# The product that subtracts the row maximum issued ahead of one projection piece or tail product in each quarter of a turn

## The chip, the cores and the metric

The kernel runs on one core of one Trainium2 chip. The metric is the device time of the whole program in microseconds (us), the median of several executions.

## The reference, cut to what matters

Two blocks are added to a residual stream of 16 x 256 tokens with 128 channels. The part that this case is about is the stack of six local-attention layers in the first block:

```python
for i in range(DEPTH):                       # DEPTH = 6, HEADS = 16, DIM_HEAD = 64, WINDOW = 32
    x = attn_layer(shift_tokens(x), Wqkv[i], q_scale[i], k_scale[i], Wo[i]) + x
    x = ffn_layer(shift_tokens(x), ln_g[i], ln_b[i], W1[i], b1[i], W2[i], b2[i]) + x

# attn_layer
q, k, v = jnp.split(x @ Wqkv, 3, -1)         # per head: q, k normalised, scaled, rotated
sim = jnp.einsum('bhwie,bhwje->bhwij', bq, bk2) * QK_SCALE      # window of 32 against 64 keys
sim = jnp.where(mask, -jnp.finfo(sim.dtype).max, sim)
attn = jax.nn.softmax(sim, -1)
out = jnp.einsum('bhwij,bhwje->bhwie', attn, bv2)
```

The softmax subtracts the maximum of each row before the exponential. The rest (a feature-map attention before these layers, a linear attention and eight experts behind them) is computed by other phases of the kernel, which the change doesn't touch.

## The kernel before

**Phases.** `features_phase`, then `layers_phase`, then the mixing and experts phase. `layers_phase` is written by hand in raw engine queues: each engine executes its list in order, and semaphores tie the lists together. A wait stands in front of the instruction that needs it, so everything behind it on the same engine waits too.

**Turns and quarters.** `turns` runs `turn(layer, j)` for 6 layers x 16 batches, 96 turns in steady work, with a few turns at the start and at the end that are partly empty. A turn works on several batches at once: it projects batch j+1, attends for batch j (and the tail of j-1), and runs the feed-forward of batches j-2 and j-3. It has four quarters; each handles one "group" (128 queries x 8 heads) at three stages of attention. I number the quarters 0 to 3, as the index of `gs`, `gt` and `ga` in the code.

**What PE does in a quarter.** `score` (L295 mask product, L304 the score products) for group gs, `probs_t` (L321) for group ga, `q_t` (L277) for group gt, then one piece of other work, then `shift` (L312) for gs, `pv` (L333) for ga, `k_t` (L286) for gt, `out_t` (L342) for ga, and between them further pieces. The piece that stands between `q_t` and `shift` is

- quarter 0: `k0`, six projection products (L221 to L223),
- quarter 1: `q1`, six projection products, and `mean` (L366),
- quarter 2: `hidden2`, two products of the feed-forward (L388),
- quarter 3: `wo_first`, the first half of the output projection (L351). It waits for `resid2`, which DVE raises in `finish` (L862).

**How the row maximum travels.** DVE's `row_max` (L762) waits for the scores and writes the negated maxima `neg_max`. PE's `shift` waits for it (`nmax`) and adds them to the scores in PSUM with a product against the identity. ACT's `exps` (L540) waits for `shifted`. The probabilities are used one quarter later, by `probs_t` and by DVE's `row_sum` (L768). `pv` in the same quarter belongs to the previous group; it needs `probs_t_out` (ACT, L547), not this quarter's exponential.

**DVE's order in a quarter.** `cosines` (L738, waits for ACT's squares L502), in quarter 1 also `normalize` (L849), `row_max`, in quarter 3 `finish` (L862), in quarter 2 two `glu` (L855), then `row_sum`, `sines` (L748), `norm_out` (L778, waits for `pv`), `sum_squares` (L756). At the end of the turn stands the Newton chain for reciprocal square roots (`newton`) and `rstd_diag` (L825). At the turns next to the end of a layer, `divide` (L714 to L716) splits the next layer's weights on DVE as well.

Of the kernel before, what the change touches and what calls it, by code (L numbers as in the profile page):

```python
# [43 lines left out]
def after(eng, sem, count):  # L44

    if not isinstance(count, int) or count > 0:
        eng.wait_ge(sem, count)
# [19 lines left out]
def layers_phase(nc, layer_qk, layer_w, consts, XF):  # L67

    ctx = ExitStack()
    with ctx:  # L70
# [75 lines left out]
        def more(layer):  # L146

            return not isinstance(layer, int) or layer < DEPTH - 1
# [64 lines left out]
        def _(pe):  # L213
            mm = nc.tensor.matmul

            def project(m, t, x, bank, done):

                for half in range(2):
                    out, o = bank[:, 512 * half:512 * half + 512], x * INNER + 512 * half
                    hi, lo = XHI[m.p][:, t * P:(t + 1) * P], XLO[m.p][:, t * P:(t + 1) * P]  # L220
                    mm(out, hi, HI[:, o:o + 512], start=True, stop=False)  # L221
                    mm(out, hi, LO[:, o:o + 512], start=False, stop=False)  # L222
                    last = mm(out, lo, HI[:, o:o + 512], start=False, stop=True)  # L223
                last.then_inc(done, 1)
# [9 lines left out]
            def k0(m):  # L234

                if m.live:
                    after(pe, rot, m.n * 8)
                    project(m, 0, 1, PJ[1], proj_qk)

            def q1(m):  # L240

                if m.live:
                    pe.wait_ge(rot, m.n * 8 + 2)
                    after(pe, v_out, m.n * 2)
                    project(m, 1, 0, PJ[0], proj_qk)
# [9 lines left out]
            def v0(m):  # L255

                if m.live:
                    pe.wait_ge(rot, m.n * 8 + 6)
                    project(m, 0, 2, PJ[0], proj_v)
# [10 lines left out]
            def q_t(g):  # L270

                if g.live:
                    pe.wait_ge(scaled, g.n + 1)
                    after(pe, kt_out, g.n * 2)
                    for c in range(4):
                        o = (4 * g.half + c) * P
                        last = nc.tensor.transpose(TP[:, c * P:(c + 1) * P], U[g.m.p][:, g.t, 0, o:o + P], IDENT[:])  # L277
                    last.then_inc(tq_mm, 1)

            def k_t(g):  # L280

                if g.live:
                    pe.wait_ge(qt_out, g.n + 1)
                    for c in range(4):
                        o = (4 * g.half + c) * P
                        last = nc.tensor.transpose(TP[:, c * P:(c + 1) * P], U[g.m.p][:, g.t, 1, o:o + P], IDENT[:])  # L286
                    last.then_inc(tk_mm, 1)

            def score(g):

                if not g.live:
                    return
                base = TILE0 - WIN if g.t == 0 else HALO
                after(pe, exped, g.n)
                mm(S[:].rearrange("p (c k) -> p c k", k=P), IDR[:], MASKR[:, g.t:g.t + 1, :].broadcast_to([P, 4, P]), start=True, stop=False,  # L295
                   skip_group_check=True)
                pe.wait_ge(qt_out, g.n + 1)
                pe.wait_ge(kt_out, g.n * 2 + 2)
                if g.t == 1:
                    pe.wait_ge(halo, g.m.n * 2 + g.half + 1)  # L300
                for c in range(4):
                    for w in range(4):
                        q, k = g.t * P + WIN * w, base + WIN * w
                        last = mm(S[WIN * w:WIN * w + WIN, c * P:(c + 1) * P], QT[:, 4 * g.half + c, q:q + WIN],  # L304
                                  KD[:, :, 4 * g.half + c, k:k + 2 * WIN], start=False, stop=True, skip_group_check=True)
                last.then_inc(scores, 1)

            def shift(g):

                if g.live:  # L310
                    pe.wait_ge(nmax, g.n + 1)
                    mm(S[:].rearrange("p (a e) -> p a e", e=DH), IDR[:], NMX[:].unsqueeze(2).broadcast_to((P, 8, DH)), start=False, stop=True,  # L312
                       skip_group_check=True).then_inc(shifted, 1)

            def probs_t(g):

                if g.live:
                    pe.wait_ge(exped, g.n + 1)
                    after(pe, ot_out, g.n)
                    for c in range(4):  # L320
                        last = nc.tensor.transpose(A[:, c * P:(c + 1) * P], E[:, g.k % 2, c * P:(c + 1) * P], IDENT[:])  # L321
                    last.then_inc(pt_mm, 1)

            def pv(g):

                if not g.live:
                    return
                pe.wait_ge(pt_out, g.n + 1)
                pe.wait_ge(v2_in, g.m.n * V2DMA + (V2TILE0 if g.t == 0 else V2DMA))
                for c in range(4):  # L330
                    for w in range(4):
                        o = c * P
                        last = mm(A[WIN * w:WIN * w + WIN, o:o + P], PT[:, o + WIN * w:o + WIN * w + WIN],  # L333
                                  V2[:, 4 * g.t + w, :, 4 * g.half + c, :], start=True, stop=True)
                last.then_inc(pv_mm, 1)

            def out_t(g):

                if g.live:
                    pe.wait_ge(o_norm, g.n + 1)  # L340
                    for c in range(4):
                        last = nc.tensor.transpose(A[:, c * P:(c + 1) * P], O[:, c * P:(c + 1) * P], IDENT[:])  # L342
                    last.then_inc(ot_mm, 1)
# [40 lines left out]
            def hidden(m, j):  # L384

                for r in range(2):
                    k = r * HCH + j
                    last = mm(W1B[j][:, r * N:(r + 1) * N], W[:, O_W1 + k * P:O_W1 + (k + 1) * P], XN[:], start=True, stop=True)  # L388
                last.then_inc(w1_mm, 1)
# [9 lines left out]
            def hidden2(m, varied):  # L399

                if m.live:
                    if varied.live:
                        pe.wait_ge(arg_ln, varied.n + 1)
                    hidden(m, 2)
# [12 lines left out]
            def turn(layer, j):  # L417
                now, n1, n2 = Batch(layer, j), Batch(layer, j + 1), Batch(layer, j + 2)
                w, e, h = Batch(layer, j - 1), Batch(layer, j - 2), Batch(layer, j - 3)
                gt, gs, ga = ([Group(layer, j, s - d) for s in range(4)] for d in (1, 2, 3))  # L420

                score(gs[0])
                probs_t(ga[0])
                q_t(gt[0])
                if j == B - 1 and more(layer):
                    pe.wait_ge(split, layer * 6 + 10)
                k0(n1)
                shift(gs[0])
                pv(ga[0])
                k_t(gt[0])  # L430
                out_t(ga[0])
                v1(now, n1)
                rstd_rows(h, e)

                score(gs[1])
                probs_t(ga[1])
                q_t(gt[1])
                q1(n1)
                mean(e)
                shift(gs[1])  # L440
                pv(ga[1])
                k_t(gt[1])
                out_t(ga[1])
                if j == 3 and (not isinstance(layer, int) or layer > 0):
                    pe.wait_ge(w_in, layer * 16 + 16)
                hidden01(h, n1)
                variance(e)

                score(gs[2])
                probs_t(ga[2])  # L450
                q_t(gt[2])
                hidden2(h, e)
                shift(gs[2])
                pv(ga[2])
                k_t(gt[2])
                k1(n1, h)
                mix(h)
                out_t(ga[2])
                if j == B - 1 and more(layer):
                    pe.wait_ge(split, layer * 6 + 12)  # L460
                v0(n1)

                score(gs[3])
                probs_t(ga[3])
                q_t(gt[3])
                if j == B + 1 and more(layer):
                    pe.wait_ge(wo_in, layer * 16 + 32)
                wo_first(w)
                shift(gs[3])
                pv(ga[3])  # L470
                k_t(gt[3])
                if j == B - 2 and more(layer):
                    pe.wait_ge(split, layer * 6 + 8)
                q0(n2)
                out_t(ga[3])
                wo_second(w)
# [1413 lines left out]
```

## Time and profile before

| | us |
|---|---|
| median of 3 runs (5209.8 to 5212.44) | 5211.34 |
| the profiled execution, its own time | 5219.45 |
| its span in the trace | 5217.7 |
| of it: before the layers | about 950 |
| of it: the layers | about 3593 |
| of it: behind the layers | about 674 |
| one regular turn of the layers | 37.10 |

The page's slices show PE with 9 tenths or more from the first fifth of the span to its last tenth, and the granted TensorE clock close to full there. POOL has the long waits; DVE and ACT are each busy about seven to eight tenths of a turn. A regular turn begins with the mask product L295 of quarter 0; the turn that starts at 2391.7 us is the one read below. A matmul's duration is modelled and overlaps the next one: the distance from one start to the next is what it takes of PE, 0.23 us for a 512-column product in a row of such (2394.64, 2394.87 and 2395.11 us are the starts of three).

### The profile page before, as it was taken

What the parts mean: (1) busy time and instruction counts of PE and PEld (TensorE: products, weight loads), DVE (VectorE), ACT (ScalarE), POOL (GpSimd) and SP (SyncE); (2) the same over time, 40 slices, a digit from 0 to 9 for tenths busy, and PEclk for the clock granted to TensorE, in tenths of its full rate; (3) what the DMA queues carried; (4) which work ended last, traced back from release to release, by engine and by line L of the source; (5) the groups of instructions that cost most, each with busy time, mean ns of one, the idle gap of its engine ahead of it and who ended that gap; (6) DMA issues with size and microseconds to landing.
All of it is one profiled execution on the core that took longest, in us unless ns stands there. A gap on an engine that the chain in (4) does not pass through costs nothing. (4 is left out here: it accounts for less than half of the span.)

```text
span 5217.7 us, 120602 instructions
## 1 busy us (share of the span) xinstructions
PE 4808.6 (92%) x45392; PEld 3485.4 (67%) x45392; DVE 3688.8 (71%) x6774; ACT 3189.9 (61%) x5142; POOL 1795.6 (34%) x966
## 2 busy tenths in 40 slices
PE   6888886799999999999999999999999999869999
PEld 2333332577777777777777777777777777648788
DVE  5665664777777777777777777777777777655554
ACT  4666664576766766666766676666666666523333
POOL 0000000545445454444544555445444454200000
PEclk9999998899999999999999999999999999979999
DMA  0000000222222222222212222222222222110000
GB/s 24 7 6 12 6 4 32 60 54 55 55 68 63 55 54 55 71 60 54 56 49 75 55 55 54 70 60 54 55 54 77 54 55 54 40 43 9 8 6 4
DMA packets 133931, 232.27 MB, mean 45 GB/s; under 512 B 29208, under 2 KB 33952, under 8 KB 132128
## 3 DMA queue, kind: packets, MB, share of 16 engines
q1 hardware_dynamic: 133408, 225.16, 16.5%
q8 instruction: 344, 5.64, 0.4%
q14 instruction: 179, 1.47, 0.1%
HBM read 32.11 MB, written 4.19 MB: 7 GB/s over the span
## 5 line engine op out<-in xcount | busy, mean ns | idle before, releaser
L660 POOL TENSOR_TENSOR qk_rotated<-qk_rotated,rotary_sines 128x1024 f32<-128x1024 f32 x384 | 913.1, 2378 | 1383.8 <-DVE rotary_sines L748 1383.8
L671 POOL TENSOR_TENSOR qk_rotated<-qk_rotated,rnorm 128x1024 f32<-128x1024 f32 x384 | 747.3, 1946 | 405.1 <-DVE rnorm L814 397.7
L738 DVE TENSOR_TENSOR qk_rotated<-ps_proj,rotary_scaled 128x1024 f32<-128x1024 f32 x384 | 469.6, 1223 | 275.4 <-ACT qk_squared L502 262.1
L523 ACT ACTIVATE k_t_by_head<-ps_qk_t 64x512 f32<-64x512 f32 x768 | 453.9, 591 | 239.0 <-PE ps_qk_t L286 229.7
L221 PE MATMUL ps_proj<-qkv_w_hi,x_shifted_hi 128*128 128x512 f32 x1152 | 504.0, 438 | 37.4 <-DVE qkv_w_lo L716 24.1
L502 ACT ACTIVATE qk_squared<-ps_proj 128x1024 f32<-128x1024 f32 x384 | 393.6, 1025 | 187.9 <-DVE qk_sumsq L756 154.3
L756 DVE TENSOR_REDUCE qk_sumsq<-qk_squared 128x16 f32<-128x1024 f32 x384 | 464.6, 1210 | 0.0
L223 PE MATMUL ps_proj<-qkv_w_hi,x_shifted_lo 128*128 128x512 f32 x1152 | 456.5, 396 | 0.0
L222 PE MATMUL ps_proj<-qkv_w_lo,x_shifted_hi 128*128 128x512 f32 x1152 | 452.1, 392 | 0.0
L748 DVE TENSOR_TENSOR rotary_sines<-ps_proj,rotary_scaled 128x1024 f32<-128x1024 f32 x384 | 450.7, 1174 | 0.0
L540 ACT ACTIVATE probs<-ps_scores 128x512 f32<-128x512 f32 x384 | 229.6, 598 | 341.6 <-PE ps_scores L312 340.4
L547 ACT ACTIVATE probs_t<-ps_attention 128x512 f32<-128x512 f32 x384 | 227.9, 593 | 316.6 <-PE ps_attention L321 316.6
L333 PE MATMUL ps_attention<-v_by_window,probs_t 128*32 128x128 f32 x12288 | 416.6, 276 | 2.0 <-ACT probs_t L547 0.2
L304 PE MATMUL ps_scores<-k_t_by_head,q_t 128*32 128x128 f32 x12288 | 415.0, 276 | 1.4 <-ACT k_t_by_head L523 1.4
L333 PEld LDWEIGHTS ps_attention<-v_by_window,probs_t 128*32 128x32 f32 x12288 | 313.1, 110 | 133.1 <-issue 91.6
L778 DVE TENSOR_TENSOR attn_out<-ps_attention,row_rsum 128x512 f32<-128x512 f32 x384 | 264.4, 689 | 187.6 <-PE ps_attention L333 187.4
L304 PEld LDWEIGHTS ps_scores<-k_t_by_head,q_t 128*32 128x32 f32 x12288 | 312.1, 109 | 125.0 <-issue 125.0
L1586 ACT ACTIVATE e_hidden<-e_ps_hidden,e_b_in 128x512 f32<-128x512 f32 x256 | 175.3, 687 | 341.7 <-PE e_ps_hidden L1541 341.5
L762 DVE TENSOR_REDUCE neg_max<-ps_scores 128x8 fp32r<-128x512 f32 x384 | 263.1, 685 | 111.9 <-PE ps_scores L304 111.8
L687 POOL MEMSET v_by_window<- 128x8192 f32 x1 | 6.9, 6925 | 899.1 <-POOLq L992 899.1
L342 PE MATMUL ps_attention<-ident,attn_out 128*128 128x128 f32 x1536 | 242.0, 280 | 46.4 <-DVE attn_out L778 46.3
L1152 PE MATMUL f_ps_attn<-f_features,f_kv 128*32 128x256 f32 x1024 | 244.4, 382 | 39.1 <-ACT f_features L1246 28.3
(239 smaller groups left out, 10461.4 us busy)
## 6 DMA issues: line engine op xcount, KB each, us to landing
v_by_window<-v_tokens SPq DMA_DIRECT2D x1152, 128.0 KB, 2.4
v_by_window<-v_tokens SPq DMA_DIRECT2D x384, 64.0 KB, 2.1
v_by_window<-v_by_window SPq DMA_DIRECT2D x192, 64.0 KB, 2.0
qkv_w_raw<-in_layer_qk_dram SPq DMA_DIRECT2D x7, 1664.0 KB, 7.5
layer_w<-in_layer_w_dram SPq DMA_DIRECT2D x6, 580.5 KB, 3.8
layer_w<-in_layer_w_dram SPq DMA_DIRECT2D x6, 512.0 KB, 3.7
f_x<-in_x_dram SPq DMA_DIRECT2D x8, 256.0 KB, 2.7
f_x_tail<-in_x_dram SPq DMA_DIRECT2D x8, 256.0 KB, 3.3
```

What stands on the lines that cost most here:

```text
L221: mm(out, hi, HI[:, o:o + 512], start=True, stop=False)
L222: mm(out, hi, LO[:, o:o + 512], start=False, stop=False)
L223: last = mm(out, lo, HI[:, o:o + 512], start=False, stop=True)
L304: last = mm(S[WIN * w:WIN * w + WIN, c * P:(c + 1) * P], QT[:, 4 * g.half + c, q:q + WIN], KD[:, :, 4 * g.half + c, k:k + 2 * WIN], start= ...
L333: last = mm(A[WIN * w:WIN * w + WIN, o:o + P], PT[:, o + WIN * w:o + WIN * w + WIN], V2[:, 4 * g.t + w, :, 4 * g.half + c, :], start=True, ...
L502: a(SQ[:], PJ[i % 2][:], ACT.Square).then_inc(squared, 1)
L523: a(KD[r, h, 4 * g.half:4 * g.half + 4, base:base + P], TP[r, :].rearrange("p (c k) -> p c k", k=P), ACT.Copy).then_inc(kt_out, 1)
L660: tt(u, u, TB[:], ALU.add).then_inc(added, 1)
L671: tt(u, u, r.unsqueeze(3).broadcast_to((P, 2, 8, DH)), ALU.mult).then_inc(scaled, 1)
L738: tt(U[m.p][:, t, x, :].rearrange("p (h e) -> p h e", e=DH), PJ[b][:].rearrange("p (h e) -> p h e", e=DH), cos, ALU.mult).then_inc(rot, 1)
L748: tt(TB[:].rearrange("p (h a b) -> p h a b", a=2, b=DH // 2), swapped(b), sin, ALU.mult).then_inc(rot, 1)
L756: nc.vector.reduce_sum(SS[:, 16 * i:16 * i + 16], SQ[:].rearrange("p (h e) -> p h e", e=DH), AX).then_inc(sumsq, 1)
```

## The change

In each quarter of `turn` on PE, `shift(gs[s])` is moved from behind the piece (`k0`; `q1` and `mean`; `hidden2`; `wo_first`) to right behind `q_t`. The waits that belong to the pieces (`split` and `wo_in` at the layers' borders) stay in front of them and so come behind `shift` too. No instruction is added or removed, and the other engines' lists are the same word for word.

```diff
                 q_t(gt[0])
+                shift(gs[0])
                 if j == B - 1 and more(layer):
                     pe.wait_ge(split, layer * 6 + 10)
                 k0(n1)
-                shift(gs[0])
                 pv(ga[0])
...
                 q_t(gt[1])
+                shift(gs[1])
                 q1(n1)
                 mean(e)
-                shift(gs[1])
                 pv(ga[1])
...
                 q_t(gt[2])
+                shift(gs[2])
                 hidden2(h, e)
-                shift(gs[2])
                 pv(ga[2])
...
                 q_t(gt[3])
+                shift(gs[3])
                 if j == B + 1 and more(layer):
                     pe.wait_ge(wo_in, layer * 16 + 32)
                 wo_first(w)
-                shift(gs[3])
                 pv(ga[3])
```

PE's list in quarter 0 before, from the score products to the transposes of k: `ps_scores<-neg_max` is the shift, `ps_proj` the piece `k0`, `ps_attention<-v_by_window` is `pv`.

```order
401 L304 MATMUL ps_scores<-k_t_by_head,q_t 32x128 x16
402 L321 MATMUL ps_attention<-ident,probs 128x128 x4
403 L277 MATMUL ps_qk_t<-ident,qk_rotated 128x128 x4
404 L221 MATMUL ps_proj<-qkv_w_hi,x_shifted_hi 128x512
405 L222 MATMUL ps_proj<-qkv_w_lo,x_shifted_hi 128x512
...
409 L223 MATMUL ps_proj<-qkv_w_hi,x_shifted_lo 128x512
410 L312 MATMUL ps_scores<-neg_max,ident_r 128x512
411 L333 MATMUL ps_attention<-v_by_window,probs_t 32x128 x16
412 L286 MATMUL ps_qk_t<-ident,qk_rotated 128x128 x4
```

The same place after:

```order
401 L304 MATMUL ps_scores<-k_t_by_head,q_t 32x128 x16
402 L321 MATMUL ps_attention<-ident,probs 128x128 x4
403 L277 MATMUL ps_qk_t<-ident,qk_rotated 128x128 x4
404 L312 MATMUL ps_scores<-neg_max,ident_r 128x512
405 L221 MATMUL ps_proj<-qkv_w_hi,x_shifted_hi 128x512
406 L222 MATMUL ps_proj<-qkv_w_lo,x_shifted_hi 128x512
...
410 L223 MATMUL ps_proj<-qkv_w_hi,x_shifted_lo 128x512
411 L333 MATMUL ps_attention<-v_by_window,probs_t 32x128 x16
412 L286 MATMUL ps_qk_t<-ident,qk_rotated 128x128 x4
```

The shift now has only the 8 transposes L321 and L277 between itself and the scores, where six projection products stood as well. Quarter 1 reads the same, with `mean` behind the projection in turns where it is live.

PE's list in quarter 3 before; `ps_tail<-attn_out_t` is the piece `wo_first`:

```order
455 L304 MATMUL ps_scores<-k_t_by_head,q_t 32x128 x16
456 L321 MATMUL ps_attention<-ident,probs 128x128 x4
457 L277 MATMUL ps_qk_t<-ident,qk_rotated 128x128 x4
458 L351 MATMUL ps_tail<-attn_out_t,layer_w 128x256 x4
459 L312 MATMUL ps_scores<-neg_max,ident_r 128x512
460 L333 MATMUL ps_attention<-v_by_window,probs_t 32x128 x16
```

and after:

```order
455 L304 MATMUL ps_scores<-k_t_by_head,q_t 32x128 x16
456 L321 MATMUL ps_attention<-ident,probs 128x128 x4
457 L277 MATMUL ps_qk_t<-ident,qk_rotated 128x128 x4
458 L312 MATMUL ps_scores<-neg_max,ident_r 128x512
459 L351 MATMUL ps_tail<-attn_out_t,layer_w 128x256 x4
460 L333 MATMUL ps_attention<-v_by_window,probs_t 32x128 x16
```

Here the shift moves ahead of the product that waits for DVE's `finish`.

## Rows read from the trace of the kernel before

**Rows 1.** Stretches: us, busy us by engine, granted clock, DMA, GB/s; layers, one turn.
```profile
950.00:4543.00 3593.00, 3453.63 (x38863) 2705.08 (x38862) 2766.46 (x4897) 2428.45 (x3911) 1766.91 (x951) 1.00 0.23 58
...
2391.70:2428.80 37.10, 36.09 (x407) 28.34 (x406) 28.75 (x52) 25.47 (x41) 18.58 (x10) 1.00 0.22 55
```

**Rows 2.** Timeline, quarter 0: start us, us, engine, line; in brackets idle before, releaser.
```profile
2394.10 0.47 PE L221 MATMUL ps_proj<-qkv_w_hi,x_shifted_hi 128*128 128x512 f32 x1
...
2394.42 0.68 DVE L762 TENSOR_REDUCE neg_max<-ps_scores 128x8 fp32r<-128x512 f32 x1
...
2395.33 0.39 PE L223 MATMUL ps_proj<-qkv_w_hi,x_shifted_lo 128*128 128x512 f32 x1
...
2395.56 0.38 PE L312 MATMUL ps_scores<-neg_max,ident_r 128*128 128x512 f32 x1
...
2395.84 1.17 DVE L748 TENSOR_TENSOR rotary_sines<-ps_proj,rotary_scaled 128x1024 f32<-128x1024 f32 x1
...
2395.87 1.08 PE L333 MATMUL ps_attention<-v_by_window,probs_t 128*32 128x128 f32 x32
...
2397.02 0.69 DVE L778 TENSOR_TENSOR attn_out<-ps_attention,row_rsum 128x512 f32<-128x512 f32 x1
```

**Rows 3.** Timeline, quarter 1.
```profile
2402.69 0.69 DVE L762 TENSOR_REDUCE neg_max<-ps_scores 128x8 fp32r<-128x512 f32 x1
...
2402.74 0.47 PE L221 MATMUL ps_proj<-qkv_w_hi,x_shifted_hi 128*128 128x512 f32 x1
...
2404.44 0.57 PE L312 MATMUL ps_scores<-neg_max,ident_r 128*128 128x512 f32 x1
...
2404.94 1.08 PE L333 MATMUL ps_attention<-v_by_window,probs_t 128*32 128x128 f32 x32
```

**Rows 4.** Timeline, quarter 2.
```profile
2411.12 0.68 DVE L762 TENSOR_REDUCE neg_max<-ps_scores 128x8 fp32r<-128x512 f32 x1
...
2411.76 1.03 PE L388 MATMUL ps_tail<-y_normed,layer_w 128*128 128x256 f32 x4
...
2413.03 0.81 PEld L333 LDWEIGHTS ps_attention<-v_by_window,probs_t 128*32 128x32 f32 x32 [0.43 <-ACT probs_t L547]
...
2413.34 0.50 ACT L583 ACTIVATE gate<-ps_tail,layer_w 128x256 f32<-128x256 f32 x1
```

**Rows 5.** Timeline, quarter 3.
```profile
2420.68 0.69 DVE L762 TENSOR_REDUCE neg_max<-ps_scores 128x8 fp32r<-128x512 f32 x1 [1.09 <-PE ps_scores L304]
...
2421.28 0.48 DVE L862 SCALAR_TENSOR_TENSOR stream<-ps_tail,layer_w,stream 128x256 f32<-128x256 f32 x1
...
2421.82 1.99 PE L351 MATMUL ps_tail<-attn_out_t,layer_w 128*128 128x256 f32 x8 [0.18 <-DVE stream L862]
...
2423.46 0.57 PE L312 MATMUL ps_scores<-neg_max,ident_r 128*128 128x512 f32 x1
...
2423.95 1.08 PE L333 MATMUL ps_attention<-v_by_window,probs_t 128*32 128x128 f32 x32
...
2425.10 0.69 DVE L778 TENSOR_TENSOR attn_out<-ps_attention,row_rsum 128x512 f32<-128x512 f32 x1 [1.42 <-PE ps_attention L333]
```

**Rows 6.** All instructions of L312: what PE sat idle for, us, times.
```profile
  DVE neg_max L762: 64.9, 51
```

**Rows 7.** Timeline, quarter 0 of two turns at layer borders.
```profile
2093.04 0.68 DVE L762 TENSOR_REDUCE neg_max<-ps_scores 128x8 fp32r<-128x512 f32 x1
...
2093.78 0.19 PEld L312 LDWEIGHTS ps_scores<-neg_max,ident_r 128*128 128x128 f32 x1 [2.31 <-DVE neg_max L762]
...
2695.75 0.48 PE L312 MATMUL ps_scores<-neg_max,ident_r 128*128 128x512 f32 x1 [1.88 <-DVE neg_max L762]
2696.16 1.83 PE L333 MATMUL ps_attention<-v_by_window,probs_t 128*32 128x128 f32 x32
```

**Rows 8.** Stretches around these two, columns as in the first group.
```profile
2085.00:2100.00 15.00, 12.68 (x146) 9.58 (x144) 13.27 (x28) 6.60 (x11) 6.53 (x4) 1.00 0.16 40
...
2680.00:2700.00 20.00, 17.93 (x196) 13.98 (x195) 16.27 (x34) 8.30 (x14) 8.68 (x4) 0.91 0.13 34
```

## The prediction, made before the changed kernel had run

> **What bounds the kernel now.** I read the page first, for the engine that is busy longest, which is PE, and then the stretches: the layers take 3593 us of the span, with PE busy 3453.63 of them and the clock granted in full, and a regular turn is 37.10 us with PE busy 36.09 [rows 1]. There is little idle time on PE, so the turn lasts as long as PE's list, and a microsecond that PE waits anew is a microsecond of the turn, unless a wait that it has anyway shrinks by it. DVE, with 28.75 us a turn, is not the bound, but its list is in order, and in several places PE needs what stands in the middle of it. Last I read one turn's timeline quarter by quarter, since the four quarters differ in one thing: when DVE delivers the row maximum, seen against the moment at which PE is through with `q_t`. That moment is the start of the first product of the piece, because the piece follows `q_t` without a wait (quarter 3 apart).
>
> **Quarter 0.** PE starts `k0` at 2394.10. DVE's `row_max` runs from 2394.42 to 2395.10 [rows 2]; it is late because the Newton chain and `cosines` stand ahead of it. Today the shift starts at 2395.56, without a wait: `k0` covers the lateness. After the change PE reaches the shift where `k0` starts now, and waits. A shift that waited starts 0.06 us behind the end of `row_max` (such a wait stands in [rows 7]: 2093.04 + 0.68 = 2093.72, and a start at 2093.78), that is at 2395.16. The delay is 2395.16 - 2394.10 = 1.06 us. The products behind it are the same in number, in another order, so `pv`, now at 2395.87, comes 1.06 later. Who waits for that: DVE's `norm_out`, which starts at 2397.02, just as `sines` is done (2395.84 + 1.17 = 2397.01) and `pv` too (2395.87 + 1.08 = 2396.95). It has no slack for a later `pv`: it moves by 1.06, and `out_t`, the square sums, and ACT's squares behind them with it. **Term: +1.06.**
>
> **Quarter 1.** `row_max` ends at 2402.69 + 0.69 = 2403.38, a shift behind it starts at 2403.44; PE is through with `q_t` at 2402.74, where `q1` starts [rows 3]. Delay 0.70 us. Today `q1` and `mean` cover it: the shift goes at 2404.44, `pv` at 2404.94. The start of this `row_max` hangs on DVE's and ACT's chain from `pv` of quarter 0 (`norm_out`, square sums, ACT's squares, `cosines`), and PE's list to `q_t` hangs on the same `pv`; both move together, so the wait of quarter 0 doesn't pay for this one. **Term: +0.70.**
>
> **Quarter 2.** `row_max` ends at 2411.80, a waiting shift starts at 2411.86, and the piece `hidden2` at 2411.76 [rows 4]: a wait of 0.10. But `pv` waits here already, 0.43 us, for ACT's `probs_t_out`, which this doesn't move. `hidden2` itself comes 0.10 and one product (0.23, below) later, so it ends at 2413.12 instead of 2412.79; ACT takes up its gate at 2413.34, so that is covered. **Term: 0**; if the cover were gone, +0.1.
>
> **Quarter 3.** `row_max` ends at 2421.37, and `finish`, which `wo_first` waits for, at 2421.28 + 0.48 = 2421.76 [rows 5]. So the shift can go at 2421.43 while PE waits for `finish` anyway, and `wo_first` starts at 2421.82 as before. From the shift's start to that of `pv` passes 0.49 here, 0.50 in quarter 1 and 0.31 in quarter 0 [rows 2, 3, 5], and a product in a row takes 0.23 (from 2395.33 to 2395.56 [rows 2]): the last product of `wo_first` is still draining in the 0.49. What falls out of the path is one product. `pv` comes 0.23 us earlier (bounds 0.2 and 0.49), and `norm_out`, which waited 1.42 us for it, follows. **Term: -0.23.**
>
> **ACT.** `exps` may start 0.4 to 2.0 us earlier (in quarter 3 behind 2421.43 instead of behind 2423.46). That is worth nothing by itself: the probabilities are taken up a quarter later, and ACT's next work behind `exps` is `k_t_out`, which waits for `k_t` on PE, behind `pv`. In quarter 2 `exps` stands behind the gate and its table load and was not waiting for the shift at all.
>
> **The borders of the layers.** In some two turns of each layer DVE splits weights too, and the row maximum is later still: PE waits for it there already, up to 2.31 us [rows 7]; over the whole run, with its partly empty turns, such waits make 64.9 us in 51 places [rows 6]. The piece that ran ahead of that wait now runs behind it. Its length is 2395.56 - 2394.10 = 1.46 in quarter 0 [rows 2]; part of it is hidden by DVE's own `row_sum` and `sines`, so I take 1.1 to 1.2, which is the same as in a regular turn. There is one thing more. In the turn at 2695 us, PE had been idle 1.88 us and the granted clock of that stretch is 0.91, with `pv` at 1.83 us instead of 1.08; in the turn at 2093 us, after the same kind of wait, it stayed at 1.00 [rows 7, 8]. Such waits become 1.5 us longer, so that a fall to 1.2 GHz should be the rule at these borders, not the exception. From 1.83 - 1.08 a fall costs 0.75 us or so; for six to eight more of them 5 us.
>
> **The sum.** A regular turn: 1.06 + 0.70 + 0 - 0.23 = 1.53 us, which makes it 38.6 instead of 37.1. Times 96 turns: 147 us, at the borders 5 more, less 2 for the partly empty turns: +150 us. Against the profiled execution's own time, 5219.45, that gives 5369; this execution lies 8 us above the median of the runs. For the median: 5211.34 + 150 = 5361 us, 2.9% slower.
>
> **A rule that speaks of the same thing.** The Trainium skill, in "Perfetto Trace Analysis", section "Matmul Optimizations", says that the engine scales its power with its utilisation, so that matmuls should run back to back in batches. The trace agrees as far as the 0.91 above shows it, at one border. Taken strictly it would make each of the new waits dangerous, the regular ones of 1.06 and 0.70 us too; that is the rival on the clock below.
>
> **Rivals.**
> *The waits are absorbed in part.* PE has waits of its own: 0.43 ahead of `pv` in quarter 2, 0.18 ahead of `wo_first` in quarter 3 [rows 4, 5]. If their releasers kept their time while PE came later, they would swallow up to 0.61 of the 1.76 us a turn. It speaks against it that each releaser is itself released by PE after the delayed `pv`: `norm_out`, square sums, squares and table load in one case, scores, `row_max` and `finish` in the other. Time: 1.53 - 0.61 = 0.92 a turn, 88 us in all, 5300 us. Chance 0.11.
> *The clock falls in regular turns too.* PE would then have an idle stretch of about 1.1 us in every turn and 0.7 in another. In the trace there are waits of 1.2 to 1.9 us in the layers after which the stretch stayed at 1.00, as [rows 8] show for one. If every second turn lost 0.75 us, that were 36 us more: 5397 us. Chance 0.08.
> *Faster.* The one mechanism that gives time back is quarter 3's. It decides the sign if the maxima arrive before PE is through with `q_t`: then no quarter waits, and 0.23 us a turn stays, -22 us, 5189 us. It is so from a `row_max` that ends 1.06 us earlier in quarter 0 and 0.70 earlier in quarter 1. DVE would have to have `row_max` ready ahead of `cosines`, and its list is unchanged, so I give it 0.02.
> *No effect.* The delay of PE would have to be met everywhere by slack behind `pv`; or the product that waits would not hold up what stands behind it. Both are against the lists in order. 5211 us. Chance 0.01.
>
> **How the numbers follow.** The forecast, 5361, has 0.78; within it the terms can be off by 0.1 each (quarter 2 uncovered, quarter 3 between 0.2 and 0.49, the borders between 0 and 15 us), which makes 5335 to 5385. To hold 8 in 10 with the rivals on either side I take 5320 to 5390. About 0.2% is what a measurement of this kernel can tell from no change; slower by more than that has the forecast and the first two rivals, 0.97; within it 0.01; faster 0.02.
>
> **What would show it.** In the trace after, in a regular turn: 38.6 us from one L295 of quarter 0 to the next; ahead of L312 idle time of PE released by DVE L762, about 0.6 to 1.0 us in quarter 0 and 0.3 to 0.7 in quarter 1 (the modelled tail of `q_t` hides a part), almost none in quarters 2 and 3; `norm_out` in quarters 0 and 1 waiting for `pv` 1.0 and 1.1 us; in quarter 3 L312 ahead of L351, which starts right behind the end of L862. The numbers of L312's waits should rise from 51 places to about 200. The forecast is wrong if the turn is under 38.2 us although these waits are there (then something absorbed them), or if the waits are there in the size forecast and the clock of the layers is below 1.00 in regular turns.

## The result: 3.3% slower

The changed kernel takes 5383.48 us (median of 4 runs, 5380.66 to 5386.61) against 5211.58 us before: a ratio of 1.033, 95% interval 1.0313 to 1.0348, or 172 us more. The forecast was 5361 us, 150 more, in a range of 5320 to 5390. The profiled execution took 5380.66 us.

### The profile page after: what moved, and what is told of

The parts are those of the page before. It is cut to its first block and busy times, and to the rows that moved or that the text cites. A ratio compares the mean times of both kernels' runs of the same rounds, so it can differ in the third digit from the quotient of the medians.

```text
span 5378.9 us, 120602 instructions
## 1 busy us (share of the span) xinstructions
PE 4854.7 (90%) x45392; PEld 3497.5 (65%) x45392; DVE 3699.9 (69%) x6774; ACT 3170.5 (59%) x5142; POOL 1792.7 (33%) x966
## 3 DMA queue, kind: packets, MB, share of 16 engines
HBM read 32.11 MB, written 4.19 MB: 7 GB/s over the span
## 5 line engine op out<-in xcount | busy, mean ns | idle before, releaser
L221 PE MATMUL ps_proj<-qkv_w_hi,x_shifted_hi 128*128 128x512 f32 x1152 | 491.6, 427 | 34.7 <-DVE qkv_w_lo L716 24.1
L312 PE MATMUL ps_scores<-neg_max,ident_r 128*128 128x512 f32 x384 | 186.7, 486 | 170.9 <-DVE neg_max L762 170.9
```

## The profile after, read as before

The stretches first: the layers, and one regular turn (columns as in [rows 1]).

```profile
950.00:4710.00 3760.00, 3502.58 (x38852) 2717.78 (x38852) 2776.01 (x4896) 2407.73 (x3910) 1762.46 (x950) 0.99 0.22 56
2418.90:2457.60 38.70, 36.54 (x408) 28.39 (x407) 28.83 (x52) 25.25 (x41) 18.56 (x10) 1.00 0.21 52
```

The turn is 38.70 us where it was 37.10, and no engine does more in it: DVE has 28.83 for 28.75, ACT 25.25 for 25.47. PE's products are the same; its 36.54 for 36.09 us busy goes by modelled ends. The time is idle time. Which, the waits in the layers tell (us in total, times, longest):

```profile
ACT k_t_by_head L523 <- PE ps_qk_t L286: 546.7, 290, 4.9
DVE attn_out L778 <- PE ps_attention L333: 299.3, 289, 3.6
PE ps_scores L312 <- DVE neg_max L762: 170.9, 202, 3.3
```

Before, the last of them was 27.5 us in 25 places in the layers (PE's products alone; [rows 6] counts the weight loads too), and DVE's wait for `pv` 187.4 us in 198. PE now waits for the row maximum, and ACT and DVE wait longer for what stands behind that wait on PE. The timeline of the regular turn shows where. Quarter 0, which answers [rows 2]:

```profile
2420.92 0.60 PE L277 MATMUL ps_qk_t<-ident,qk_rotated 128*128 128x128 f32 x4
2421.59 0.68 DVE L762 TENSOR_REDUCE neg_max<-ps_scores 128x8 fp32r<-128x512 f32 x1
...
2422.33 0.48 PE L312 MATMUL ps_scores<-neg_max,ident_r 128*128 128x512 f32 x1 [0.81 <-DVE neg_max L762]
...
2424.13 1.08 PE L333 MATMUL ps_attention<-v_by_window,probs_t 128*32 128x128 f32 x32
...
2425.28 0.69 DVE L778 TENSOR_TENSOR attn_out<-ps_attention,row_rsum 128x512 f32<-128x512 f32 x1 [1.09 <-PE ps_attention L333]
```

The shift starts 0.06 us behind the end of `row_max` (2421.59 + 0.68 = 2422.27) and has waited 0.81 us by the modelled ends. `norm_out`, which started without idle time before, now waits 1.09 us. Quarter 1, which answers [rows 3]:

```profile
2430.55 0.60 PE L277 MATMUL ps_qk_t<-ident,qk_rotated 128*128 128x128 f32 x4
2430.95 0.69 DVE L762 TENSOR_REDUCE neg_max<-ps_scores 128x8 fp32r<-128x512 f32 x1
...
2431.69 0.48 PE L312 MATMUL ps_scores<-neg_max,ident_r 128*128 128x512 f32 x1 [0.54 <-DVE neg_max L762]
```

Quarter 2, to be held against [rows 4]: the wait of the shift is there, 0.16 us on its weight load, and the one ahead of `pv` has shrunk from 0.43 to 0.33.

```profile
2440.84 0.19 PEld L312 LDWEIGHTS ps_scores<-neg_max,ident_r 128*128 128x128 f32 x1 [0.16 <-DVE neg_max L762]
...
2442.11 0.81 PEld L333 LDWEIGHTS ps_attention<-v_by_window,probs_t 128*32 128x32 f32 x32 [0.33 <-ACT probs_t L547]
```

Quarter 3, against [rows 5]: the shift runs while DVE is still at `finish`, and `wo_first` starts 0.06 us behind the end of that (2450.29 + 0.47), with no idle time on PE itself.

```profile
2450.29 0.47 DVE L862 SCALAR_TENSOR_TENSOR stream<-ps_tail,layer_w,stream 128x256 f32<-128x256 f32 x1
2450.43 0.48 PE L312 MATMUL ps_scores<-neg_max,ident_r 128*128 128x512 f32 x1
2450.82 1.99 PE L351 MATMUL ps_tail<-attn_out_t,layer_w 128*128 128x256 f32 x8
2452.75 1.08 PE L333 MATMUL ps_attention<-v_by_window,probs_t 128*32 128x128 f32 x32
```

The distance from one mask product (L295) to the next is the length of a quarter. Here are its medians over the run, and beside them the same for the experiments told below:

| kernel | quarter 0 | 1 | 2 | 3 | turn |
|---|---|---|---|---|---|
| before | 8.158 | 9.531 | 9.808 | 9.627 | 37.12 |
| after | 9.255 | 10.259 | 9.806 | 9.404 | 38.72 |
| moved in quarter 0 alone | 9.259 | 9.530 | 9.809 | 9.620 | 38.22 |
| in quarter 1 alone | 8.168 | 10.246 | 9.808 | 9.625 | 37.85 |
| in quarter 2 alone | 8.159 | 9.527 | 9.808 | 9.625 | 37.12 |
| in quarter 3 alone | 8.168 | 9.517 | 9.809 | 9.402 | 36.90 |
| after, row maximum early in 0 | 8.226 | 10.255 | 9.806 | 9.397 | 37.68 |
| after, early in 0 and 1 | 8.213 | 9.537 | 9.812 | 9.398 | 36.96 |
| before, finish first | 8.168 | 9.528 | 9.810 | 9.171 | 36.68 |

What is beyond the regular turns lies at the borders of the layers. Four kinds of quarter are longer there than the median; summed over the first five layers, in us:

| excess of | before | after |
|---|---|---|
| quarter 0 of the turn of the layer's last batch (j = 15) | 13.9 | 19.6 |
| quarter 0 of the loop body's first turn (j = 3; 0.2 in layer 0, before and after) | 7.0 | 14.7 |
| quarters 2 of turns 14 and 15 | 11.9 | 15.7 |
| falls of the granted clock in the layers, number | 3 | 9 |

That is 17 us. With 1.60 us in each of 96 turns, 154 us, it makes 171 of the 172. One place more is longer: quarter 0 of turn 11 of the last layer, 1.9 us before and 4.3 after, with one of the nine falls; the partly empty turns take as much back, so that over all quarters the excess grows by 16.9 us. Of the three falls before, one lies in the first turns and two in the turns with j = 15.

Only at j = 15 is DVE late in quarter 0 because it has split weights. At j = 3 no weight is split, and DVE stands idle ahead of `cosines`. In the third layer, before the change:

```profile
2243.42 0.60 PE L277 MATMUL ps_qk_t<-ident,qk_rotated 128*128 128x128 f32 x4
...
2244.99 1.23 DVE L738 TENSOR_TENSOR qk_rotated<-ps_proj,rotary_scaled 128x1024 f32<-128x1024 f32 x1 [3.43 <-PE ps_qk_t L277]
```

The profile puts the wait down to L277, which is over by 2244.02; what holds DVE for the last 0.97 us is not shown.

## The experiments

Each kernel was compared with the kernel before in runs on the same chip; its median there lay between 5214.2 and 5214.7 us. Differences below are against that.

### One quarter at a time

Four kernels, each the kernel before with one of the four moves, as in quarter 3:

```diff
                 q_t(gt[3])
+                shift(gs[3])
                 if j == B + 1 and more(layer):
                     pe.wait_ge(wo_in, layer * 16 + 32)
                 wo_first(w)
-                shift(gs[3])
```

> The shift is moved in quarter 0 alone. Theory A (each quarter has a price of its own, and the rest is paid at the layer borders): quarter 0 grows by 1.09 us, 105 us in 96 turns, and with it come the border turns, where the wait ahead of the shift is already there and the clock then falls, some 20 us: 5336 us, and 9 or so falls of the granted clock in the layers. Theory B (the quarters are coupled: a wait in one moves or swallows that of the next): the four kernels with one move each don't add up to the 172 us of the changed kernel, by more than 15 us.

> The shift is moved in quarter 1 alone. Theory A: 0.73 us a turn, +70 us, 5282 us, no more falls of the clock than before. Theory B: less than 0.5 us a turn here, since without the wait of quarter 0 DVE would be further ahead, or more than 0.9.

> The shift is moved in quarter 2 alone. Theory A: the wait of 0.1 us lies in the one that pv has for ACT's copy, so a regular turn keeps 37.1 us; the two border turns of each layer in which this row maximum is 1.7 us late may cost 0.5 us each. 5211 to 5217 us. Theory B: a gain or loss above 0.1 us a turn, outside 5201 to 5221.

> The shift is moved in quarter 3 alone. Theory A: it goes while PE waits for DVE's finish, and one product falls out of the path: 0.22 us a turn, -21 us, 5190 us, a regular turn of 36.9 us. Theory B: the 0.22 us seen in the changed kernel came from the slack that the other quarters' waits made, and alone it gives less than 0.1 us a turn, above 5201 us.

| moved in | us | difference | ratio, interval |
|---|---|---|---|
| quarter 0 | 5330.55 | +116.4 | 1.0226 (1.0209 to 1.0243) |
| quarter 1 | 5284.91 | +70.7 | 1.013 (1.0113 to 1.0147) |
| quarter 2 | 5215.95 | +1.8 | 1.0003 (0.9993 to 1.0013) |
| quarter 3 | 5196.61 | -17.6 | 0.9963 (0.9949 to 0.9977) |

The four differences sum to 171.3 us; the changed kernel has 171.9. That they meet within 1 us is luck, since the interval of each is 5 to 9 us to either side. What carries the reading is the table of quarters: each move changes its own quarter and leaves the other three within 0.014 us. So theory A holds and B falls: each wait has a price of its own, and none pays for another. By A's numbers quarter 0 came out 9 us low (116 for 125, with 6 falls of the clock, not 9), and quarter 3 gave 18 instead of 21 us: 0.22 in 96 turns is 21, and at the borders the clock fell five times instead of twice. In quarter 2 the 3.8 us of the two border turns are in the trace (excess 15.7 for 11.9), and the measured 1.8 can't be told from nothing.

### The borders

> The changed kernel, but in quarter 0 of two turns of each layer (the first of the loop's body, and the one before the layer's last) the shift keeps its old place. There DVE is late by 2.4 to 3.5 us. In the changed kernel these quarters are longer than regular ones by 19.6 and 14.7 us in all against 13.9 and 7.0 in the kernel before. If the part of the cost above 96 times the regular price is paid there: the 13.4 us come back, and the regular 1.09 us of some 11 quarters with them, 24 us: 5359 us, with falls of the clock as in the kernel before (3). If it is paid elsewhere: 5372 us (the regular price of 11 quarters alone), and still 9 falls.

```diff
+                if j != 3 and j != B - 1:
+                    shift(gs[0])
                 k0(n1)
-                shift(gs[0])
+                if not (j != 3 and j != B - 1):
+                    shift(gs[0])
```

Measured: 5356.86 us, ratio 1.0272 (1.0254 to 1.0289), 27 us under the changed kernel, or 29 as differences to the kernel before; 24 were expected, 11 would have meant that the extra is paid elsewhere. So these 11 quarters carried 15 to 17 us beyond their regular price of 12. The clock falls 5 times in the layers, where 3 were expected: four times at the quarters with the old order, which had two falls in the kernel before, and once in turn 11 of the last layer, which keeps the new order.

Is it the clock, or the place of the piece behind the late maximum? For this PE got work inside the wait:

> The changed kernel, but in the same quarters PE computes the six products of k0 once more ahead of the shift, into the bank that k0 then overwrites: 1.46 us of work inside a wait of some 3 us, so that PE idles there no longer than in the kernel before. Theory clock (what the borders cost more is the fall of the granted clock behind a long wait): the falls go from 9 to 3 or 4, the excess of these quarters back towards 2.4 and 1.6 us each, some 10 us in all: 5372 us. Theory place (it is the piece that stands behind the late maximum): no change, 5383 us, however the clock behaves.

```diff
+                if j == 3 or j == B - 1:
+                    if j == B - 1 and more(layer):
+                        pe.wait_ge(split, layer * 6 + 10)
+                    warm(n1)
                 shift(gs[0])
-                if j == B - 1 and more(layer):
-                    pe.wait_ge(split, layer * 6 + 10)
                 k0(n1)
```

`warm` computes the six products of `k0` into the same bank and raises no semaphore.

Measured: 5373.13 us, ratio 1.0309 (1.0291 to 1.0327), 10 us less than the changed kernel, or 13 as differences, and 4 falls of the clock. The two intervals touch (1.0313 to 1.0348 for the changed kernel), so the times alone don't decide between the theories; the quarters do. Six products more in 11 turns cost nothing and seem to have made the kernel faster. The timeline of one such quarter in the changed kernel, at the border of the first turn of [rows 7], shows what they save:

```profile
2142.73 0.68 DVE L762 TENSOR_REDUCE neg_max<-ps_scores 128x8 fp32r<-128x512 f32 x1
...
2143.47 0.48 PE L312 MATMUL ps_scores<-neg_max,ident_r 128*128 128x512 f32 x1 [3.28 <-DVE neg_max L762]
...
2144.72 0.59 PE L222 MATMUL ps_proj<-qkv_w_lo,x_shifted_hi 128*128 128x512 f32 x1
...
2145.66 1.94 PE L333 MATMUL ps_attention<-v_by_window,probs_t 128*32 128x128 f32 x32
...
2147.66 0.69 DVE L778 TENSOR_TENSOR attn_out<-ps_attention,row_rsum 128x512 f32<-128x512 f32 x1 [2.33 <-PE ps_attention L333]
```

and the same quarter with the extra products (L323 is the shift, L775 `row_max`, L344 `pv`, L791 `norm_out`):

```profile
2140.03 0.68 DVE L775 TENSOR_REDUCE neg_max<-ps_scores 128x8 fp32r<-128x512 f32 x1
...
2140.76 0.48 PE L323 MATMUL ps_scores<-neg_max,ident_r 128*128 128x512 f32 x1 [1.89 <-DVE neg_max L775]
...
2142.55 1.08 PE L344 MATMUL ps_attention<-v_by_window,probs_t 128*32 128x128 f32 x32
2143.70 0.69 DVE L791 TENSOR_TENSOR attn_out<-ps_attention,row_rsum 128x512 f32<-128x512 f32 x1 [1.07 <-PE ps_attention L344]
```

From the shift to `norm_out` pass 4.19 us in the one and 2.94 in the other. The granted clock of 15 us around these quarters, in the same order:

```profile
2135.00:2150.00 15.00, 11.72 (x109) 8.91 (x108) 12.08 (x27) 4.97 (x9) 6.38 (x4) 0.89 0.06 13
```

```profile
2132.00:2147.00 15.00, 12.88 (x120) 9.78 (x118) 13.10 (x27) 5.43 (x10) 6.69 (x4) 1.00 0.10 25
```

In the changed kernel PE had been idle 3.28 us, the clock fell to 1.2 GHz 1.3 us after PE had work again, and `pv` took 1.94 us instead of 1.08. With the extra products the idle time is 1.89 and it stayed at 2.4 GHz. Where it stays, the excess of this quarter over a regular one is 2.45 us, as good as the 2.36 of the kernel before; in the two of five borders where it falls all the same, the excess is 4.0. The one border of the changed kernel at which the clock stayed has 2.45 too, without any extra product. The theory of the clock expected 5372 us and that of the place 5383: the clock has it, though the falls that are left (2 of the 5 borders at j = 15, one at j = 3; the fourth, in turn 11 of the last layer, had no extra products) show that the extra products don't prevent all of them. The kernel with the move in quarter 0 alone says the same of j = 3: with the shift in the same place, but without a fall, these five quarters have an excess of 9.0 us, and with four falls, in the changed kernel, 14.7.

### The lateness of the maximum, taken away

If the waits are all there is, an earlier maximum must give back the quarters 0 and 1 although the shift stays in its new place.

> The changed kernel, and on DVE row_max of quarter 0 ahead of cosines. The maxima then end near 2394.06 on the old timeline, and PE is through with q_t at 2394.10. If the price of quarter 0 is the lateness of the maximum alone: the 1.09 us a turn go, 105 us, and some of the borders' cost: 5270 us, quarter 0 at 8.2 us again. If it is something else (where the shift stands relative to k0, or DVE's later cosines now hold up what follows): 5330 us or more.

> The changed kernel, and on DVE row_max ahead of cosines in quarters 0 and 1 (in quarter 1 ahead of normalize as well). In quarter 1 of the kernel before the scores end at 2401.47, so the maximum could end at 2402.23 and the shift go at 2402.29, ahead of 2402.74, when PE is through with q_t; cosines would begin at 2402.23 instead of 2401.22, but DVE has 0.46 us of slack ahead of norm_out and gives back 0.69 for row_max. If the lateness of the maximum is all: 0.73 us a turn less than with quarter 0 alone, 70 us from 5275: 5205 us, quarter 1 at 9.53. If the later cosines hold up something: quarter 1 stays above 9.8 us and the time above 5235.

```diff
-                cosines(n1, 0)
                 row_max(gs[0])
+                cosines(n1, 0)
...
+                row_max(gs[1])
                 cosines(n1, 1)
                 normalize(h)
-                row_max(gs[1])
```

The first of these (quarter 0 alone) took 5275.39 us, ratio 1.0111 (1.0094 to 1.0128): 110.8 of the 171.9 us are gone, where 105 and some of the borders were expected. Both together took 5206.36 us, ratio 0.9987 (0.9978 to 0.9997), 69.4 us less again, for 70 expected. Quarter 1 of the second, with the shift in front of `q1` as in the changed kernel:

```profile
2359.56 0.69 DVE L762 TENSOR_REDUCE neg_max<-ps_scores 128x8 fp32r<-128x512 f32 x1 [1.49 <-PE ps_scores L304]
2360.17 1.22 DVE L738 TENSOR_TENSOR qk_rotated<-ps_proj,rotary_scaled 128x1024 f32<-128x1024 f32 x1
2360.29 0.60 PE L277 MATMUL ps_qk_t<-ident,qk_rotated 128*128 128x128 f32 x4
...
2360.64 0.46 PE L312 MATMUL ps_scores<-neg_max,ident_r 128*128 128x512 f32 x1
```

The maximum is done at 2360.25, before PE is even at `q_t`, and the shift runs without a wait. So the place of the shift costs next to nothing (0.05 us in quarter 0 and 0.01 in quarter 1 are left, and the later `cosines` may be that); its being ahead of its input costs the rest.

### Quarter 3: what the gain was

> The kernel before with the old order on PE, and on DVE finish ahead of row_max in quarter 3, in the 1.09 us in which DVE waits for the scores. If quarter 3's gain is that the shift fills PE's wait for finish: the wait itself goes here, 0.35 us a turn (wo_first at 2421.47 instead of 2421.82), 33 us: 5178 us, more than the 18 us of the move. If the gain came from the exponential that starts earlier, or from something else: no gain here, 5211 us.

```diff
-                row_max(gs[3])
                 finish(h)
+                row_max(gs[3])
```

Measured: 5169.44 us, ratio 0.9917 (0.99 to 0.9933), 44.8 us less. The forecast was 33; the quarter is 9.171 us, 0.456 under the kernel before, where I had reckoned 0.35. The wait itself is the 0.35 (from L295 to L351 pass 2.26 us instead of 2.61); the other 0.10 lies behind it, where from L351 to `pv` pass 2.04 instead of 2.14. Its timeline, with the old order on PE:

```profile
2362.41 0.47 DVE L862 SCALAR_TENSOR_TENSOR stream<-ps_tail,layer_w,stream 128x256 f32<-128x256 f32 x1
...
2363.59 0.69 DVE L762 TENSOR_REDUCE neg_max<-ps_scores 128x8 fp32r<-128x512 f32 x1 [0.71 <-PE ps_scores L304]
...
2363.95 0.60 PE L277 MATMUL ps_qk_t<-ident,qk_rotated 128*128 128x128 f32 x4
...
2364.39 1.89 PE L351 MATMUL ps_tail<-attn_out_t,layer_w 128*128 128x256 f32 x8
...
2365.93 0.57 PE L312 MATMUL ps_scores<-neg_max,ident_r 128*128 128x512 f32 x1
```

`finish` takes the place of idle time that DVE had ahead of the scores (the rest of it is the 0.71), and `wo_first` follows `q_t` without a gap. From the start of L277 to that of L351 pass 0.44 us, and 0.78 with the shift between them in the changed kernel.

> Both ways at once in quarter 3: finish ahead of row_max on DVE, and the shift ahead of wo_first on PE; all else as before. If both earn the same thing, PE's wait for finish: no sum, the time of finish first alone, 5169 us, quarter 3 at 9.17. If they earn different things: 18 us less, 5151 us, quarter 3 at 8.95.

> The changed order on PE with row_max early in quarters 0 and 1 and finish ahead of row_max in quarter 3. PE then waits for no maximum in a regular turn, and the place of the shift should be worth nothing: 8.23 + 9.53 + 9.81 + 9.17 = 36.74 us a turn, against 36.68 for finish first with the old order, 5175 us. If the early shift has a use of its own (exponentials, and with them the other queues, earlier): under 5165 us.

The two ways in quarter 3 at once took 5177.96 us, ratio 0.993 (0.9913 to 0.9946): no sum, and 8 us more than `finish` first alone. Quarter 3 is 9.226 us, 0.055 more than with the old order, since the maximum is ready just too late for the first place: the shift's weight load starts at 2.21 us of the quarter, the one of `wo_first` in that place at 2.15. With `row_max` early in quarters 0 and 1 as well it is 5189.97 us, ratio 0.9953 (0.9936 to 0.9969), 15 more than expected and 20 more than `finish` first with the old order. The turn is 36.78 us, 0.10 more than there, which is 10 us; the other 10 lie at the borders, where the excess of the same four kinds of quarter is 10 us larger, with 5 falls of the clock there for 2. An early shift showed no use of its own, then; where the maximum is late in rare turns, it loses.

The kernel before with `finish` first is the fastest of all that ran, and it leaves the shift where it was.

## Why the prediction was right

**Quarters 0 and 1** were forecast at +1.06 and +0.70 and measured +1.10 and +0.73. Each term was the end of `row_max` less the moment at which PE is through with `q_t`, and the single moves show the two prices alone. The 0.03 to 0.04 each lie behind the wait: from the shift to `pv` pass 1.80 us in quarter 0, and I had 1.77.

**Quarter 2** was forecast at 0 and measured 0.00: the new wait is there and is taken out of the one ahead of `pv`.

**Quarter 3** was forecast at -0.23 and measured -0.22, and the reason held: with PE's wait for `finish` removed in another way, the move earns nothing.

**That nothing absorbs the waits** held in the lengths of the quarters. Each wait on PE that looked as if it had room hangs on the same `pv`: the wait of `norm_out` grew by the delay of PE, and PE's own wait for `norm_out` (0.23 us, quarter 0) is 0.23 after the change too.

**The borders** are the step that was mis-sized. I put in 5 us for falls of the clock, with 0.75 us each from the length of one `pv`, and took off 2 for the partly empty turns. The excess grew by 17 us. The number of falls was right: eight in the quarters of turns 3 and 15 where two were before, and one in turn 11 of the last layer. Their size wasn't: in the quarter of turn 15 the excess is 2.45 us without a fall and 3.7 to 4.8 with one, so that a fall costs 1.3 to 2.4, since it lasts beyond `pv`. In the order before a fall cost 1.0 to 1.2 us in its own quarter, of which the next one gave 0.45 back; there the 0.75 would have been about right. With 2.45 at each turn 15, and the 9.0 that turn 3 has without falls, the eight falls make 13 us. And quarter 2 of turns 14 and 15, where the maximum is late as well and `hidden2` now stands behind it, costs 0.38 us each (1.63 for 1.25, 1.51 for 1.13), which I had left at nothing. From 150 to 172, the regular turns have 0.07 us times 96, 7 us, and the borders the rest. The reason that I gave for the late maximum, the splitting of weights, holds for turn 15 and not for turn 3.

**The rival on the clock** in regular turns didn't come: the regular turn has 1.00 with waits of 0.81 and 0.54 us in it. The signs named in advance were there: L312's waits rose from 25 places to 202, and `norm_out` in quarter 0 waits 1.09 us. The 51 that I started from was a misreading: [rows 6] counts a wait once for the weight load and once for the product, and counted like that it rose to 474. In quarter 1 the 1.1 us forecast are there as well, but in two parts, since `center`, ahead of it on DVE, waits for PE's `mean`, which has become late too: 0.48 + 0.62.

```profile
2434.03 0.42 DVE L842 TENSOR_TENSOR y_centered<-y_shifted,ps_tail 128x256 f32<-128x256 f32 x1 [0.48 <-PE ps_tail L366]
2435.07 0.69 DVE L778 TENSOR_TENSOR attn_out<-ps_attention,row_rsum 128x512 f32<-128x512 f32 x1 [0.62 <-PE ps_attention L333]
```

The rule of the Trainium skill ("Perfetto Trace Analysis", "Matmul Optimizations"), that power follows utilisation, has its evidence at the borders alone.

## What to carry to other kernels

On an engine whose list is in order, an instruction that waits should stand just behind the work that covers the lateness of its input. Its price in an earlier place is read from one turn: the end of its input less the moment at which the engine would reach it, and nothing if the engine waits in that place anyway for something else. Before an instruction is moved into such a wait, see whether the wait can be removed at its source: here the reordering of two DVE instructions gave 45 us, the move into the wait 18. And read the rare turns too: the input was latest at the layers' borders, and in the changed kernel the clock fell at most of the long waits there.

## What the runs showed of the hardware

A wait of PE of 1.9 to 3.3 us brought the clock to 1.2 GHz in some turns and not in others, and the longest most often. Ahead of the shift in quarter 0 of turn 15, five such waits in each of the thirteen kernels:

| wait | kernels | clock fell |
|---|---|---|
| 1.9 us | 8 | 22 of 40 |
| 2.15 us (`row_max` early in quarter 0) | 3 | 7 of 15 |
| 3.28 us (changed kernel, quarter 0 alone) | 2 | 9 of 10 |

The length of the wait doesn't decide alone. With the move in quarter 0 alone, the four long waits at j = 3, of 2.6 to 3.4 us, passed without a fall; in the changed kernel all four, of 2.1 to 3.0 us, had one. One of the former, with the granted clock of the 15 us around it:

```profile
2283.34 0.48 PE L312 MATMUL ps_scores<-neg_max,ident_r 128*128 128x512 f32 x1 [3.40 <-DVE neg_max L762]
2276.00:2291.00 15.00, 10.62 (x134) 7.61 (x132) 9.10 (x19) 4.67 (x9) 6.36 (x3) 1.00 0.17 43
```

By the granted clock in the traces, five of the nine falls in the changed kernel began 0.7 to 1.3 us after PE had work again, so that the whole slow stretch lies on the work behind the wait. The other four began 0.7 to 0.9 us before the wait ended, and they lasted twice as long; they are the costly ones (excess 4.8 us at turn 15, against 3.7 to 3.8). One of these, at the first turn 15:

```profile
1510.57 0.80 PE L312 MATMUL ps_scores<-neg_max,ident_r 128*128 128x512 f32 x1 [3.28 <-DVE neg_max L762]
1510.00:1516.00 6.00, 5.43 (x41) 3.82 (x42) 2.54 (x5) 0.60 (x1) 4.03 (x3) 0.50 0.00 0
```

What sets the moment of a fall, no run here shows. Giving PE work that nobody needs in such waits, which made them 1.9 us again, took the falls from nine to four and the time down by 10 to 13 us.
